# A quantised feed-forward: the first activation and product ahead of the shift and rounding, and the ternary down weights turned inside its first two row tiles

## The reference, cut to what matters

```python
def _quant_weight(w):
    scale = jnp.mean(jnp.abs(w)) + EPS
    wq = jnp.clip(jnp.round(w / scale), -1.0, 1.0)
    return (wq, scale)

def _quant_act(x):
    s = jnp.max(jnp.abs(x), axis=-1, keepdims=True) / 127.0 + EPS
    xq = jnp.clip(jnp.round(x / s), -128.0, 127.0)
    return (xq, s)

def _qlinear(x, w):
    wq, ws = _quant_weight(w)
    xq, xs = _quant_act(x)
    return jnp.einsum('bsi,oi->bso', xq, wq) * xs * ws

gate = jax.nn.silu(_qlinear(x, w_gate))     # w_gate, w_up: 2048 x 512
up = _qlinear(x, w_up)
x = _layernorm(x + _qlinear(gate * up, w_down))   # w_down: 512 x 2048
```

## Time and profile before

| | us |
|---|---|
| median of 3 runs (2911.3 to 2918.1) | 2917.49 |
| the profiled execution's own time | 2918.93 |
| its span, first to last instruction | 2917.2 |
| TensorE busy | 2683.2 (92%) |
| VectorE busy | 1798.4 (62%) |
| ScalarE busy | 1422.5 (49%) |
| weight stage, first transfer to last copy | 2668.45 to 2689.50 |
| feed-forward, first activation to last instruction | 2689.90 to 2913.87 |

### The profile page before, as it was taken

How to read it: one execution, slowest core, us unless ns; L and a number is a source line. 1 busy time by engine, 2 the same in 40 slices (tenths; PEclk the granted TensorE clock), 3 DMA queues, 4 the chain that set the end, 5 groups by cost and what they waited for, 6 DMA issues and landing times. The chain is left out here.

```text
span 2917.2 us, 40519 instructions
## 1 busy us (share of the span) xinstructions
PE 2683.2 (92%) x12686; PEld 1671.8 (57%) x12686; DVE 1798.4 (62%) x3459; ACT 1422.5 (49%) x2981; POOL 288.5 (10%) x397
## 2 busy tenths in 40 slices
PE   8998998979799995999999999997999999997888
PEld 4454554444388872677677777775545454533443
DVE  5665674644443335656756756754777777874676
ACT  5453553422033332355454553653677676764554
POOL 0230003001521104000000000001110101000000
PEclk9999999989899998999999999999999999998999
DMA  4395105531587762523223223211000000002000
GB/s 151 73 114 159 43 14 166 200 131 60 164 264 239 238 210 58 195 78 126 81 102 110 73 102 116 72 73 58 6 5 6 5 6 2 2 2 88 8 22 30
DMA packets 114166, 266.24 MB, mean 91 GB/s; under 512 B 14464, under 2 KB 37008, under 8 KB 113200
## 3 DMA queue, kind: packets, MB, share of 16 engines
q1 hardware_dynamic: 97152, 211.16, 22.0%
q0 software_dynamic: 16816, 52.64, 8.1%
HBM read 208.97 MB, written 58.48 MB: 92 GB/s over the span
## 5 line engine op out<-in xcount | busy, mean ns | idle before, releaser
L2451 DVE TENSOR_REDUCE x_neg_max<-bank 128x1 f32<-128x512 f32 x512 | 327.4, 684 | 95.9 <-PE bank L2296 95.6
L2403 ACT ACTIVATE x_weights<-bank 128x512 f32<-128x512 f32 x512 | 279.1, 600 | 127.0 <-PE bank L2307 122.2
L1830 ACT ACTIVATE a_probs<-bank,a_neg_max 128x128 f32<-128x128 f32 (+3 forms) x256 | 136.2, 532 | 201.2 <-DVE a_neg_max L1924 197.0
L1730 PE MATMUL bank<-a_x_high,a_weights 128*128 128x512 f32 x640 | 218.4, 404 | 7.8 <-DVE a_x_low L1854 2.3
L109 PEld LDWEIGHTS bank<-all_ident,a_probs 128*128 128x128 f32 x1200 | 151.5, 140 | 84.3 <-issue 44.7
L109 PE MATMUL bank<-all_ident,a_probs 128*128 128x128 f32 x1200 | 193.4, 273 | 2.2 <-ACT a_probs_t L1822 2.2
L1822 ACT COPY a_probs_t<-bank 128x128 f32<-128x128 f32 (+3 forms) x256 | 107.6, 420 | 144.1 <-PE bank L109 143.9
L1765 PE MATMUL bank<-a_k_cols,a_q_cols 128*128 128x128 f32 (+3 forms) x512 | 176.7, 434 | 0.5 <-DVE a_q_cols L1873 0.3
L1794 PE MATMUL bank<-a_wo,a_att_high 128*128 128x512 f32 x512 | 162.2, 398 | 4.7 <-DVE a_q_cols L1873 2.9
L1455 DVE TENSOR_TENSOR moe_acc<-bank,moe_acc 128x512 f32 x79 | 54.7, 692 | 170.4 <-PE bank L1121 170.2
L1110 PE MATMUL bank<-moe_gh_cols,moe_item 128*128 128x256 f32 x632 | 152.0, 384 | 4.1 <-DMA moe_item<-moe_items 3.5
(11 more groups left out here) (406 smaller groups left out, 5394.3 us busy)
## 6 DMA issues: line engine op xcount, KB each, us to landing
a_weights<-split_qkv SPq DMA_DIRECT2D x80, 512.0 KB, 3.6
moe_item<-moe_items SPq DMA_DIRECT2D x79, 257.0 KB, 3.9
moe_item<-moe_items SPq DMA_DIRECT2D x79, 256.0 KB, 3.9
a_wo<-split_out SPq DMA_DIRECT2D x8, 2048.0 KB, 8.0
a_wo<-split_out SPq DMA_DIRECT2D x16, 1024.0 KB, 10.3
split_qkv<-x_qkv_parts SPq DMA_DIRECT2D x12, 1024.0 KB, 5.1
moe_items<-in_L_ffn_e_w POOLq DMA_DIRECT2D x40, 256.0 KB, 34.5
split_out<-a_turned SPq DMA_DIRECT2D x8, 1024.0 KB, 4.0
```

The costliest lines, as they stand in the source:

```text
L1730: last = pe.matmul(mm[g % 2], weight[:, k, :], x[:, k, :], start=n == 0, stop=n == 3 * KD - 1)
L1830: act.activation(probs[:, n % SLOTS, 0:t], sc[n % 4][:, 0:t], ACT.Exp, bias=neg_max[:, n:n + 1], accum_out=row_sum[:, n:n + 1]).then_inc(s ...
L2403: act.activation(weights[:, chunk % 2, k, :], weight_banks[slot % 2], ACT.Exp).then_inc(s.weight.free, 1)
L2451: dve.tensor_reduce(neg_max[:, g % 2, j, h:h + 1], score_banks[slot % 3], AX.X, ALU.max, negate=True) \
```

## The change

Two things are changed, both in the last two stages.

The down weights are loaded in the weight stage as before, but into a buffer of their own (`quant_down`), with no wait between the four transfers, and they are not turned there. TensorE turns them in the first two row tiles of the feed-forward: after each of the 8 up groups it turns two of the 16 tiles, one into each of the two banks that the down product uses from turn 2 on. ScalarE copies one of the two out behind its activation, VectorE the other behind its product.

And in each turn ScalarE does its first activation before the shift of the tile before, and VectorE its first product before it rounds the hidden rows of the tile before and normalises the tile two before that (`finish`); it was the other way round.

```diff
@@ ternary_weights
-    PARTS, PIECES = 4, 12
+    PARTS, PIECES = 4, 8
+            for c in range(PARTS):
+                sp.dma_start(w.quant_down[:, c, :].rearrange("p (g n) -> p g n", g=2),
+                             packed.ternary[2, 2 * c:2 * c + 2].rearrange("g p n -> p g n")).then_inc(w.down_in[c], 16)
...
-            for n in range(WEIGHTS * TILES):
+            for n in range(2 * TILES):
@@ ternary_ffn, TensorE, after each up group
+                        for n in turns(t, c):
+                            pe.wait_ge(w.down_in[n // 4], 16)
+                            pe.wait_ge(s.down_free[n % 2], n // 2 + 1)
+                            turn_tile(pe, mm[n % 2].bitcast(BF16), w.quant_down[:, n // 4, n % 4 * 512:(n % 4 + 1) * 512], ident_b[:], 4) \
+                                .then_inc(s.down_full[n % 2], 1)
@@ ternary_ffn, ScalarE
-                if 1 <= t <= LAST + 1:
-                    act.wait_ge(s.h_top, t)
-                    act.activation(shifted_h[:], inner[:, other, :], ACT.Identity, bias=round_col[:],
-                                   scale=inv_h[:, other:other + 1]).then_inc(s.h_shifted, 1)
+                if t == LAST + 1:
+                    shift_h(LAST, other)
                 if t <= LAST:
                     for c in range(COLS):
+                        if c == 1 and t >= 1:
+                            shift_h(t - 1, other)
                         act.wait_ge(s.ga.full, t * COLS + c + 1)
                         act.activation(gated[:, slot, c * 512:(c + 1) * 512], ga[c % 2], ACT.Silu,
                                        scale=step_gate[:, t:t + 1]).then_inc(s.ga.free, 1)
+                        for n in turns(t, c)[0:1]:
+                            act.wait_ge(s.down_full[0], n // 2 + 1)
+                            act.copy(down_rows(n), blocks_of(mm[0].bitcast(BF16), 4)).then_inc(s.down_free[0], 1)
@@ ternary_ffn, VectorE
+                if t > LAST:
+                    finish(t - 1, 1 - slot)
                 if t <= LAST:
                     for c in range(COLS):
+                        if c == 1 and t >= 1:
+                            finish(t - 1, 1 - slot)
                         dve.wait_ge(s.up.full, t * COLS + c + 1)
...
+                        for n in turns(t, c)[1:2]:
+                            dve.wait_ge(s.down_full[1], n // 2 + 1)
+                            dve.tensor_copy(down_rows(n), blocks_of(mm[1].bitcast(BF16), 4)).then_inc(s.down_free[1], 1)
...
+            def finish(t, slot):
+                if t <= LAST:
                     dve.wait_ge(s.h_shifted, t + 1)
                     if t >= 2:
                         dve.wait_ge(s.tq.full, h_bank(t - 2, 1) + 1)
                     dve.tensor_scalar(quant_h[:, slot, :], shifted_h[:], ROUND_INT, 127.0, ALU.subtract, ALU.min).then_inc(s.h_ready, 1)
                 if t >= 2:
+                    x = m.x_tok[:, t - 2, :]
                     dve.wait_ge(s.rstd_ready, t - 2 + 1)
-                    dve.tensor_scalar(x, x, st.mean_var[:, slot, 0:1], st.rstd[:, at], ALU.subtract, ALU.mult).then_inc(s.x_done, 1)
+                    dve.tensor_scalar(x, x, st.mean_var[:, slot, 0:1], st.rstd[:, slot:slot + 1], ALU.subtract, ALU.mult).then_inc(s.x_done, 1)
```

More of the change, by code:

```diff
@@ L2574, in turned @@
             i, n = divmod(n, TILES)
[L2575 to L2578, removed]
+            return (w.gate, w.up)[i][:, :, n * P:(n + 1) * P]
         def bank(n):
@@ L2590, in _ @@
                              packed.ternary[i, 2 * c:2 * c + 2].rearrange("g p n -> p g n")).then_inc(loaded[q % LOADS], 16)
+            for c in range(PARTS):
+                sp.dma_start(w.quant_down[:, c, :].rearrange("p (g n) -> p g n", g=2),
+                             packed.ternary[2, 2 * c:2 * c + 2].rearrange("g p n -> p g n")).then_inc(w.down_in[c], 16)
         @block.scalar
         def _(act):
-            for n in range(0, WEIGHTS * TILES, 2):
+            for n in range(0, 2 * TILES, 2):
                 act.wait_ge(full[0], n // 2 + 1)
@@ L2601, in _ @@
             row_steps(dve, m, row)
-            for n in range(1, WEIGHTS * TILES, 2):
+            for n in range(1, 2 * TILES, 2):
                 dve.wait_ge(full[1], n // 2 + 1)
@@ L2627, in ternary_ffn @@
     LAST = B * NT - 1
+    TURNS = KI * KD // 4
     with ExitStack() as ctx:
@@ L2633, in ternary_ffn @@
         w.down, w.scale = sb("down", [P, KI, D], BF16), m.scale
+        w.quant_down, w.down_in = sb("quant_down", [P, KD, INNER], BF16), [sem(f"down_in_{c}") for c in range(KD)]
         ternary_weights(nc, m, w, q, packed)
@@ L2644, in ternary_ffn @@
         s.tq, s.ga, s.up, s.mm = (Ring(sem, n) for n in ("tq", "ga", "up", "mm"))
+        s.down_full, s.down_free = [sem(f"down_full_{i}") for i in range(2)], [sem(f"down_free_{i}") for i in range(2)]
         s.steps_ready, s.x_shifted = sem("steps_ready"), sem("x_shifted")
@@ L2659, in h_slot, with turns, down_rows @@
             return h_bank(t - 1, half) % 2
+        def turns(t, c):
+            first = (t * COLS + c) * 2
+            return range(first, first + 2 if first < TURNS else first)
+        def down_rows(n):
+            o, k = divmod(n, KI // 4)
+            return w.down[:, 4 * k:4 * k + 4, o * P:(o + 1) * P]
         def pipeline(engine, step):
@@ L2696, in step @@
                         last.then_inc(s.up.full, 1)
+                        for n in turns(t, c):
[3 more added lines that the diff above has]
+                                .then_inc(s.down_full[n % 2], 1)
                 if t < LAST:
                     turn_x(t + 1, other)
+                if t == 2:
+                    for i in range(2):
+                        pe.wait_ge(s.down_free[i], TURNS // 2 + 1)
                 if t >= 2:
@@ L2716, in _ @@
                 pe.sem_inc(ring.free, ring.size)
+            for i in range(2):
+                pe.sem_inc(s.down_free[i], 1)
             pe.wait_ge(s.ident_made, 1)
@@ L2732, in turned_x, with shift_h @@
                 act.copy(quant_xt[:, slot, :, :], blocks_of(bank.bitcast(BF16), KD)).then_inc(s.tq.free, 1)
+            def shift_h(t, slot):
+                act.wait_ge(s.h_top, t + 1)
+                act.activation(shifted_h[:], inner[:, slot, :], ACT.Identity, bias=round_col[:],
+                               scale=inv_h[:, slot:slot + 1]).then_inc(s.h_shifted, 1)
             def step(t, slot):
                 other = 1 - slot
-                if 1 <= t <= LAST + 1:
-                    act.wait_ge(s.h_top, t)
-                    act.activation(shifted_h[:], inner[:, other, :], ACT.Identity, bias=round_col[:],
-                                   scale=inv_h[:, other:other + 1]).then_inc(s.h_shifted, 1)
+                if t == LAST + 1:
+                    shift_h(LAST, other)
                 if t <= LAST:
                     for c in range(COLS):
+                        if c == 1 and t >= 1:
+                            shift_h(t - 1, other)
                         act.wait_ge(s.ga.full, t * COLS + c + 1)
@@ L2816, in _ @@
             pipeline(dve, step)
+            finish(LAST + 2, LAST % 2)
         @block.gpsimd
```

## The result

| | before | after |
|---|---|---|
| median, us (7 runs each) | 2917.49 (2911.3 to 2920.03) | 2902.9 (2895.78 to 2906.1) |
| ratio to before | | 0.9953 (95%: 0.9941 to 0.9965) |
| span of the profiled execution | 2917.2 | 2901.1 |
| last two stages: first weight transfer to last instruction | 245.4 | 226.4 |

The change is faster by 14.6 us; 2900 was forecast, 2890 to 2910 as the range. The stretches of the new profile hold the terms of the sum. They run from the feed-forward's first activation to tile 0, tile 0 at the low clock, the rest of tile 0, tile 1, tile 2, tiles 3 to 14, tile 15's groups, and the tail. The columns are length, busy time of PE, PEld, DVE, ACT and POOL, granted clock, DMA share and GB/s.

The account below looks back on a forecast made before the run. TensorE was taken to bound the feed-forward, losing 1.80 of 13.28 us per tile to waits for ScalarE and VectorE. Terms of -15.0 -1.9 -3.9 +2.3 +0.8 = -17.7 us gave 2900 us, range 2890 to 2910.

Parts of the forecast that it names:

- The loop: Feed-forward tiles 3 to 15: TensorE's waits per tile fall from 1.80 to 0.65 us, a tile takes 12.12, -15.0 us.
- Tile 2: Feed-forward tile 2, no weights to turn: from 13.36 to TensorE's 11.47 us, -1.9 us.
- The weight stage: Stage before the feed-forward: ScalarE's 8 down copies go, the up copies end it at 2685.57, -3.9 us.
- the eighth transfer: Weight stage: lands at about 2682.0, TensorE wants it at about 2684.4, so 2.4 us of cover if served in order.
- Tile 1: Feed-forward tile 1: -0.23 to its last up group's end, with one 0.78 wait, then +1.00 behind it, +0.8 us.
- Tile 0: Feed-forward tile 0: 24 transposes add 1.34 us, the next tile's start comes 1.00 later, together +2.3 us.
- loses 2.76 whatever work falls in it, as before: Tile 0: TensorE starts at clock 0.50 for 5.52 us and loses 2.76 us, the same as before the change.
- The clock did not stay low past tile 0: Rival: clock 0.50 to tile 1's end, 2913, 5 in 100; into the fourth tile, 2930, 3 in 100.
- VectorE took over 0.65 of the wait: Rival in the loop: product 1 comes 1.15 us later than laid out, no loop gain, 2917; 5 in 100.
- None of the transfers was late: Rival in the weight stage: the eighth weight transfer lands last, 2903; 7 in 100.
- The sum: Last two stages: loop, tile 2, weight stage, tile 0 and tile 1, -15.0 -1.9 -3.9 +2.3 +0.8 = -17.7 us.

Follow-up runs that it names:

- Order alone: The new order on ScalarE and VectorE, with down weights turned in the weight stage as in the kernel before: 2906.82 us, ratio 0.9931, last two stages 227.0 us.
- two ahead: Against the changed kernel, two activations and two products ahead of shift, rounding and normalisation rather than one: 2897.08 us, ratio 0.9898 to before, last two stages 217.0.
- ScalarE's order only: The change with VectorE back in its old order, rounding and normalising ahead of its first product: 2920.26 us, ratio 1.0036 to before, last two stages 255.7.

## Why the prediction was right

- **The loop.** -15.0 was forecast for tiles 3 to 15; -13.81 (159.31 to 145.50) and -1.15 (8.71 to 7.56) were measured. The mechanism held in each experiment that moved a piece of it: 13.85, 12.85, 11.67 and 11.48 us a tile for 13.86, 12.8, 11.67 and 11.47 expected.
- **Tile 2.** -1.9 and -1.89.
- **The weight stage.** -3.9 and -3.87. TensorE did not wait for the eighth transfer, and the down weights were there in time.
- **Tile 1.** +0.8 and +0.82, with one wait before its last up group, for VectorE's copy ahead of the third pair's second tile, where it was laid out (0.78 by the layout; the row gives 0.67 of idle time).
- **Tile 0.** +2.3 and +1.0: this is the term of the sum that was mis-sized. The 24 transposes and the 1.00 behind the last up group are there (2701.22 to 2703.48 is 2.26). What failed is "loses 2.76 whatever work falls in it, as before": the low clock lasted 3.05 us and not 5.5, which loses 1.4.
- **The rivals.** The clock did not stay low past tile 0. VectorE took over 0.65 of the wait and no more. None of the transfers was late.
- **The sum** was -17.7; the stretch gave -19.1, by the 1.3 of tile 0 and 0.2 ahead of it. The medians gave 14.6, 17.8 and 19.9 in three comparisons. That the first, 2902.9, lies only 3 us from the 2900 says little by itself: the stages ahead scatter by more than that, and it is the stretches and the tiles that bear the forecast out.
- **One argument was weaker than it read.** I gave the two halves of the change as terms beside each other. Order alone has 18.4 of the 19.1 us, since tile 1 gains 1.9 from it when no weights are turned there; as a separate edit the other half is worth 0.7 on top of it, and 1.1 alone.

These are the rows of tile 1 after the change: the activation's copy holds the shift to G+2.64 (G is 2703.48), and the wait for the bank.

```profile
2705.64 0.58 ACT L2775 COPY tf_down<-bank 128x512 bf16<-128x512 bf16 x1 [0.40 <-PE bank L109]
...
2706.12 2.10 ACT L2759 ACTIVATE tf_shifted_h<-tf_inner,tf_round_col,tf_inv_h 128x2048 f32<-128x2048 f32 x1
...
2710.61 0.38 PE L109 MATMUL bank<-tf_ident_b,tf_quant_down 128*128 128x128 bf16 x4 [0.67 <-DVE tf_down L2825]
```

## What to carry to other kernels

When the busiest engine waits in a loop, write out one period of every engine from the starts in the timeline, move the instruction there, and look who is late next: this gave the period of five new orders to 0.05 us. A long instruction on data that nobody wants soon (here 2.1 us of shift) belongs behind short ones that free a bank, on both engines of a pair at once (two ahead, as many as there are banks of a kind, gave 9.3 us more than one; three was not tried); on one of them alone it can cost time. Work moved into a busy engine's "idle" gaps is worth what the gaps still hold after the other edit.

## What the hardware showed that I had not expected

With ScalarE's order only, where TensorE waits 2.4 us in each tile (by the starts; the rows give 2.2 of idle time), the clock fell within the loop: in one of twelve tiles, 1.1 us behind the end of the wait, and that tile took 1.7 us longer. Why in that one is not shown. With waits of 0.85 and 0.95 in each tile (before the change) it stayed up from tile 1 to tile 15.

A transfer queued behind others landed late: the four down transfers took 9.5 to 11.6 us from issue to landing, each with an estimated six to eight still ahead of it (one lands each 1.4 us). Yet the last came about as long after the first issue as with a wait ahead of each (19.0 and some 19.2 us).
